# Seam between two attention stages: order of maxima, key loads and the last w2 products

## What is computed

```
h1 = tanh(einsum('bshd,do->bsho', t, w1) + b1)       # t: queries, keys; 16 heads of 16
prep = einsum('bsho,on->bshn', h1, w2) + b2          # the w2 products
...
s1 = einsum('bshe,bthe->bhst', q1, k1) / 4           # q1 = x wq1, k1 = ctx wk1, by head
s2 = einsum('bshe,bthe->bhst', q2, k2) / 4
attn = softmax(s1) - gain * softmax(s2)
o = einsum('bhst,bthe->bshe', attn, ctx wv)
```

## Time and profile before

| | us |
|---|---|
| median of 3 runs | 1492.02 |
| lowest, highest | 1490.94, 1496.18 |
| the profiled execution | 1488.99 |
| its span | 1487.2 |
| TensorE, VectorE, ScalarE, GpSimd busy | 1458.0, 1139.8, 823.4, 392.0 |

### The profile page before, as it was taken

How to read it: one execution, slowest core, us unless ns; L and a number is a source line. 1 busy time by engine, 2 the same in 40 slices (tenths; PEclk the granted TensorE clock), 3 DMA queues, 4 the chain that set the end, 5 groups by cost and what they waited for, 6 DMA issues and landing times.

```text
span 1487.2 us, 28701 instructions
## 1 busy us (share of the span) xinstructions
PE 1458.0 (98%) x11013; PEld 1042.6 (70%) x11013; DVE 1139.8 (77%) x2313; ACT 823.4 (55%) x1123; POOL 392.0 (26%) x426
## 2 busy tenths in 40 slices
PE   8999999999999999999999999999999999999998
PEld 5444444435666666666567888989989898888987
DVE  6445544378999999999967888788786878788686
ACT  5887888866888888888863431323232221222221
POOL 1000111224466677566364410000000000000001
PEclk9999999999999999999999999999999999999999
DMA  7766666557656656656642201010010101110001
GB/s 152 155 116 119 117 116 126 109 88 120 109 81 111 101 82 112 100 83 97 100 155 72 78 15 34 24 29 21 22 30 15 42 17 29 29 29 15 22 22 29
DMA packets 90092, 108.83 MB, mean 73 GB/s; under 512 B 18384, under 2 KB 58524, under 8 KB 89956
## 3 DMA queue, kind: packets, MB, share of 16 engines
q1 hardware_dynamic: 89624, 106.61, 38.0%
q10 hardware_dynamic: 332, 0.39, 0.1%
HBM read 26.00 MB, written 4.19 MB: 20 GB/s over the span
## 4 chain that ended last, share of the span: by engine, by line
PE 85%; DVE 6%; ACT 2%; SPq 2%; issue 2%; POOL 1%; DMA 1%; POOLq 0%; DVEq 0%; ACTq 0%
PE ps L109 82%; PE ps L1462 2%; SPq L119 2%; ACT PX L1634 1%; ACT H L708 1%; DVE NM L1692 1%; PE ps L1424 1%; PE ps L1470 1%; POOL X L1877 0%; PE ps L1395 0%; DVE GH L2585 0%; DVE GF L2579 0%; DVE GH L2583 0%; DMA ST<-QS 0%; DMA WS<-SM 0%
## 5 line engine op out<-in xcount | busy, mean ns | idle before, releaser
L1692 DVE TENSOR_REDUCE NM<-ps 128x4 f32<-128x1024 f32 x256 | 307.5, 1220 | 23.3 <-PE ps L109 22.4
L1634 ACT ACTIVATE PX<-ps 128x1024 f32<-128x1024 f32 x256 | 262.4, 1025 | 72.2 <-PE ps L109 70.4
L708 ACT ACTIVATE H<-ps 128x1024 f32<-128x1024 f32 x240 | 229.9, 1033 | 42.8 <-PE ps L109 40.7
L2354 ACT ACTIVATE GF<-ps,cols 128x512 f32<-128x512 f32 x128 | 87.3, 688 | 222.6 <-PE ps L109 209.1
L109 PE MATMUL ps<-XC,W_sw_w 128*128 128x512 f32 x768 | 187.1, 393 | 0.0
L109 PEld LDWEIGHTS ps<-XC,W_sw_w 128*128 128x128 f32 x768 | 140.0, 188 | 27.6
L2705 POOL TENSOR_SCALAR RSc<-AGc 128x4 f32<-128x4 f32 x23 | 6.0, 260 | 570.9 <-DVE AGc L2469 570.9
L2349 ACT ACTIVATE GF<-ps 128x512 f32<-128x512 f32 x64 | 38.2, 596 | 185.0 <-PE ps L109 185.0
L2585 DVE TENSOR_TENSOR GH<-GF,GH 128x512 fp32r<-128x512 f32 x192 | 133.9, 698 | 6.6
L109 PE MATMUL ps<-PX,VT 128*32 128x256 f32 x2048 | 137.0, 385 | 0.1
L109 PE MATMUL ps<-KT,QT 48*128 48x512 f32 x512 | 127.6, 495 | 1.7 <-DVE NM L1692 0.9
(11 more groups left out here) (261 smaller groups left out, 2521.2 us busy)
## 6 DMA issues: line engine op xcount, KB each, us to landing
KT<-KS SPq DMA_DIRECT2D x128, 192.0 KB, 4.7
ST<-QS SPq DMA_DIRECT2D x254, 96.0 KB, 2.8
QT<-XSb SPq DMA_DIRECT2D x128, 96.0 KB, 4.2
XR<-TT SPq DMA_DIRECT2D x352, 32.0 KB, 1.9
XT<-in_xT_dram SPq DMA_DIRECT2D x8, 512.0 KB, 4.4
raw_a<-in_x_dram SPq DMA_DIRECT2D x8, 512.0 KB, 4.3
CR<-in_ctxT_dram SPq DMA_DIRECT2D x8, 512.0 KB, 5.7
out_dram<-X SPq DMA_DIRECT2D x7, 512.0 KB, 2.9
```

The lines of the kernel that those rows point to most:

```text
L708: e.activation(H1[s % 8][:, :, :], PP[s % 3][:, :, :], ACT.Tanh, bias=0.0 if s > 15 else b1c[:, half:half + 1], scale=1.0).then_inc(act_th, 1)
L1634: e.activation(PX[s % 3][:, :, :, :], PP[2][:, :, :].rearrange("p g (c q) -> p g c q", c=2), ACT.Exp, bias=0.0, scale=0.25).then_inc(act_e ...
L1692: e.tensor_reduce(NM[u % 2][:, qc, :, :, i], PP[qc][:, :, :].rearrange("p g (m k) -> p g m k", m=2), AX.X, ALU.max, negate=True).then_inc( ...
L2354: e.activation(g[:, :], o, f, bias=cols[:, col:col + 1], scale=1.0).then_inc(act_g, 1)
```

## The change

- In the seam the maxima lead the scores by 12 steps up to step 0 (maxima(0) at -12), by 13 from step 1 to 4, by 14 from step 5. Steps 1 and 5 have two maxima each. The reductions follow the same order.
- LAST_W2 goes from -13 to -10: the last w2 products stand behind maxima(2). The three fillers of step -11 go. prep_v(0, 0) goes from -11 to -9, where prep_x(2) stands ahead of it. The second key product of block 1 goes from -13 to -11, behind maxima(1).
- Block 1 alone has its keys split by GpSimd: ScalarE copies the product to a new tile KR, GpSimd makes the high part, the rest and the copy; VectorE has no part in it. The waits of load, prep_k and ScalarE are counted accordingly.
- rows(0) goes from step -5 to -4. put_maxima(0) goes out at -3 with one DMA from SP; ScalarE issues the other, behind its own copy.
- The loads of block 1 go from steps -7, -4, -1, 2 to -3, -2, -1, 0, all behind put_maxima(0). ones_rows(1) goes from -6 to 5 and counts on another semaphore (d_w).

```diff
--- before.py
+++ after.py
@@ -171,7 +171,7 @@
 SOON_STEPS.update({J: 14 + 2 * (J - 74) for J in range(75, 87)})
 FIRST_STEP, LATER_STEP = -52, 39
-LAST_W2 = -13
+LAST_W2 = -10
 THREES_END = 56
@@ -1009,13 +1009,15 @@
 LEAD = 14
+SECOND_LOAD = -3
 SECOND_VALUES = (25, 29, 31, 33)
 NU = 4 * NP
 NB = 2 * NP
 NS = 8 * NU
 LAST_STEP = NS + 51
-
-BUSY = {-11: 3, -10: 1, -9: 1, -8: 1, -7: 1, -6: 1, -5: 1, -4: 2, -3: 1, -2: 1}
+OWN_KEYS = (0,) + tuple(range(2, 16))
+
+BUSY = {-10: 1, -9: 1, -8: 1, -7: 1, -6: 1, -5: 1, -4: 2, -3: 1, -2: 1}
 def phase_b(M, a_end):
@@ -1064,6 +1066,7 @@
     BN = [put(f"BNb{i}", [128, 4, 6]) for i in range(2)]
     AG = [put(f"AGb{i}", [128, 4, 2]) for i in range(2)]
     RS = [put(f"RSb{i}", [128, 4]) for i in range(2)]
+    KR = put("KR", [128, TOK])
     FB = Place(M, 0)("FB", [128, 9228])
     br = Place(M, 143360)("br", [128, 3, 256])
     cols, BC, Wce, Wme = M.cols, M.BC, M.Wce, M.Wme
@@ -1143,6 +1146,13 @@
     LATE = {NP - 2: 55, NP - 1: 87}
+    def maxima_due(s):
+
+        if s <= 0:
+            return (s + LEAD - 2,) if s >= 2 - LEAD else ()
+        first = s + LEAD - (2 if s < 2 else 1 if s < 6 else 0)
+        return range(first, min(NS, s + LEAD + 1 - (1 if s < 5 else 0)))
+
     def stats_due(s):
         for p, at in LATE.items():
@@ -1201,11 +1211,25 @@
         w.wait_ge(a_end["w1"], 16 * (n + 1))
+    def copied(B):
+
+        return B not in OWN_KEYS
+
+    def own(B):
+
+        return sum(2 for b in range(B) if not copied(b))
+
+    def parts(B):
+
+        return 2 * B + 4 * sum(1 for b in range(B) if copied(b))
+
     def k_due(s):
         for m in range(2):
             B = due(s, 8 * m - 37, 16, NB)
-            if B is not None and B != 2:
+            if B is not None and B != 2 and (B, m) != (1, 1):
                 return B, m
+            if s == -11:
+                return 1, 1
             if s == 3 + 4 * m:
                 return 2, m
         return None
@@ -1220,7 +1244,7 @@
                 return p, i
         if s in SECOND_VALUES:
             return 1, SECOND_VALUES.index(s)
-        return (0, 0) if s == -11 else None
+        return (0, 0) if s == -9 else None
     def out_due(s):
@@ -1244,7 +1268,7 @@
         return due(s, 2, 2, 4 * NU)
     def rows_due(s):
-        return due(s, -5, 8, NU)
+        return {-5: None, -4: 0}.get(s, due(s, -5, 8, NU))
     def turn_n_due(s):
         return NU - 1 if s == NS + 13 else due(s, 23, 8, NU - 1)
@@ -1278,7 +1302,7 @@
                 after_stack(w, 14)
             for g in range(2):
                 dma(e, f32(KT[i][64 * g + 48:64 * g + 52, :, :, :]).rearrange("r i m t -> r i (m t)"),
-                    f32(ones[:, :, :]).rearrange("r m t -> r (m t)").unsqueeze(1).to_broadcast([4, 4, 1024]), d_ones)
+                    f32(ones[:, :, :]).rearrange("r m t -> r (m t)").unsqueeze(1).to_broadcast([4, 4, 1024]), d_w if i else d_ones)
         def load(B, i):
             p, c = B // 2, B % 2
@@ -1288,8 +1312,8 @@
                 w.wait_ge(pe_g, 1)
             if B == 1:
                 after(w, "w2")
-            w.wait_ge(pool_ks, 2 * B + 2)
-            w.wait_ge(dve_ks, 2 * B + 2)
+            w.wait_ge(pool_ks, parts(B + 1))
+            w.wait_ge(dve_ks, own(B + 1))
             w.wait_ge(pe_st, 16 * (B - 2) + 8 + 2 * i + 2)
             k, q = KT[B % 2], QT[B % 2]
             for g in range(2):
@@ -1304,7 +1328,7 @@
             q, b = QT[u // 2 % 2], u % 2
             w.wait_ge(act_nr, u + 1)
             w.wait_ge(pe_st, 8 * (u - 4) + 8)
-            for g in range(2):
+            for g in range(2 if u else 1):
                 dma(e, f32(q[64 * g + 48:64 * g + 52, :, b, :]), f32(NR[u % 2][16 * g:16 * g + 16, :]), d_mr[u % 2])
         def load_fold():
@@ -1314,7 +1338,8 @@
             w.wait_ge(pe_v, 4 * NP)
             for name in T:
                 dma(e, T[name], a[name].rearrange("(c p) n -> p c n", c=2), d_T)
-            w.wait_ge(d_ones, 80)
+            w.wait_ge(d_ones, 48)
+            w.wait_ge(d_w, 64)
             for o, name in ((vb, "vb"), (vc, "vc"), (v2, "v2"), (br[:, :, :], "br"), (cols[:, :], "cols")):
                 dma(e, o, a[name], d_V)
             dma(e, BC[:, 0, :], a["BC"][:, 0, :], d_V)
@@ -1340,17 +1365,17 @@
         def step(s):
             if s == -33:
                 first_queries()
-            u = due(s, -4, 8, NU)
+            u = rows_due(s - 1)
             if u is not None:
                 put_maxima(u)
             p = ctx_due(s)
             if p is not None:
                 load_ctx(p)
             for i in range(4):
-                B = due(s, 3 * i - 23, 16, NB)
-                if B is not None:
+                B = 1 if s == i + SECOND_LOAD else due(s, 3 * i - 23, 16, NB)
+                if B is not None and (B != 1 or s == i + SECOND_LOAD):
                     load(B, i)
-            for i, at in enumerate((-16, -6)):
+            for i, at in enumerate((-16, 5)):
                 if s == at:
                     ones_rows(i)
             if s == NS - 28:
@@ -1381,7 +1406,7 @@
             w.wait_ge(pool_c, 4 * p + 2 * c + 2)
             w.wait_ge(*free[7])
             mm3(e, P[7], G[:, m, c, 0, :], G[:, m, c, 1, :], CH[p % 2][:, c, 0, :], CH[p % 2][:, c, 1, :], True, True).then_inc(pe_k, 1)
-            free[7] = (dve_ks, 2 * B + m + 1)
+            free[7] = (act_k, 2 * B + m + 1) if copied(B) else (dve_ks, own(B) + m + 1)
         def prep_x(B):
             p, c = B // 2, B % 2
@@ -1429,7 +1454,9 @@
             u, i, m = s // 8, s % 8 // 2, s % 2
             B, b = u // 2, u % 2
             k, q = KT[B % 2], QT[B % 2]
-            w.wait_ge(d_ones, 80)
+            w.wait_ge(d_ones, 48)
+            if B:
+                w.wait_ge(d_w, 64)
             w.wait_ge(d_mr[u % 2], 32 * (u // 2 + 1))
             w.wait_ge(act_ex, s)
             for kc in range(2):
@@ -1528,8 +1555,8 @@
         def step(s):
             busy(BUSY.get(s, 0))
-            if 0 <= s + LEAD < NS:
-                maxima(s + LEAD)
+            for t in maxima_due(s):
+                maxima(t)
             if s in (0, 1):
                 busy(2, 4 + 2 * s)
             if s == 2:
@@ -1596,6 +1623,9 @@
                 w.wait_ge(pe_rows, u + 1)
                 w.wait_ge(d_mr[u % 2], 32 * (u // 2))
                 e.activation(NR[u % 2][:, :], low[0:32, :], ACT.Copy).then_inc(act_nr, 1)
+                if u == 0:
+                    w.wait_ge(act_nr, 1)
+                    dma(e, f32(QT[0][112:116, :, 0, :]), f32(NR[0][16:32, :]), d_mr[0])
             B = x_due(s - 1)
             if B is not None:
                 w.wait_ge(pe_x, B + 1)
@@ -1619,9 +1649,13 @@
             if k is not None:
                 B, m = k
                 w.wait_ge(pe_k, 2 * B + m + 1)
-                for i in range(4):
-                    w.wait_ge(d_ld[B % 2][i], 64 * ((B - 2) // 2 + 1))
-                e.activation(KS[:, B % 2, 0, m, :], P[7], ACT.Copy).then_inc(act_k, 1)
+                if copied(B):
+                    w.wait_ge(pool_ks, parts(B) + 3 * m)
+                    e.activation(KR[:, :], P[7], ACT.Copy).then_inc(act_k, 1)
+                else:
+                    for i in range(4):
+                        w.wait_ge(d_ld[B % 2][i], 64 * ((B - 2) // 2 + 1))
+                    e.activation(KS[:, B % 2, 0, m, :], P[7], ACT.Copy).then_inc(act_k, 1)
             u = due(s, 14, 8, NU)
             if u is not None:
                 w.wait_ge(pool_oc, u + 1)
@@ -1685,8 +1719,7 @@
                 after(w, "combine")
                 e.tensor_tensor(PR[:, :, 8 * f:8 * f + 8, :], v7[:, :, :, 0:16],
                                 ZR[:, :, :, :].rearrange("p q h m -> p q (h m)").unsqueeze(3).to_broadcast([128, 2, 8, 16]), ALU.mult).then_inc(dve_pr, 1)
-            t = s + LEAD
-            if 0 <= t < NS:
+            for t in maxima_due(s):
                 u, i, qc = t // 8, t % 8 // 2, t % 2
                 w.wait_ge(pe_max, t + 1)
                 e.tensor_reduce(NM[u % 2][:, qc, :, :, i], PP[qc][:, :, :].rearrange("p g (m k) -> p g m k", m=2),
@@ -1704,7 +1737,7 @@
                 w.wait_ge(pool_on, u)
                 e.tensor_reduce(VR[:, :], OQ[:, :, :], AX.X, ALU.add).then_inc(dve_vr, 1)
             k = k_due(s - 1)
-            if k is not None:
+            if k is not None and not copied(k[0]):
                 B, m = k
                 w.wait_ge(act_k, 2 * B + m + 1)
                 e.tensor_tensor(KS[:, B % 2, 2, m, :], P[7], f32(KS[:, B % 2, 0, m, :]), ALU.subtract).then_inc(dve_ks, 1)
@@ -1830,8 +1863,16 @@
             if k is not None:
                 B, m = k
                 w.wait_ge(act_k, 2 * B + m + 1)
+                hi, again, lo = (KS[:, B % 2, l, m, :] for l in range(3))
                 one.wait()
-                one.done(e.tensor_copy(KS[:, B % 2, 1, m, :], f32(KS[:, B % 2, 0, m, :])), pool_ks)
+                if copied(B):
+                    for i in range(4):
```

(6 more changed lines are left out.)

## The result

| kernel | median us (lowest to highest) | ratio to before, 95% interval |
|---|---|---|
| before | 1492.8 (1489.66 to 1496.18) | |
| changed | 1496.22 (1493.62 to 1500.77) | 1.0022 [1.0015, 1.0029] |

The change costs 3.3 us by the ratio, 0.2%, with 20 runs on each side. The profiled execution of the changed kernel took 1496.26 with a span of 1494.3; the one of before took 1488.99 with 1487.2. These two differ by 7.3, which is more than the medians do, so the first question to the traces is which part of it belongs to the change.

The account below looks back on a forecast made before the run. TensorE was taken to carry most of the chain, with VectorE's reductions and SP's queue setting the seam up to step 8. A shift of +2.0 there on the median 1492.02 gave 1494.0, range 1489.2 to 1498.0.

Parts of the forecast that it names:

- The two idles: VectorE ahead of the first row of maxima, around 323.5 and 326: waits of 1.2 and 1.35 us.
- the signs against it: In the seam: first row issued before 331.5, a block 1 load under 0.85 us, or step 8's exponential before 353.8.
- Part 1: VectorE's reductions ahead of the first row of maxima: the row is asked for some 1.0 us later.
- Part 2: Lead of 12 at the first scores: step 0 at 338.1 instead of 338.66, nothing left by step 2.
- Part 3: SP's queue, first to second row: 16 loads at 1.0 us each, second row +2.4 us; +2.0 taken at step 8.
- the bound of +4.3: Upper bound for the second row's issue in SP's queue: 353.5, if 16 loads run at 1.12 us each.
- the upper price that I named: SP's issue time per load of block 1 at the pace of the slowest stretch: 1.12 us.
- Part 4: Covered work in the seam: GpSimd's keys cost nothing, ScalarE's issue (about 0.7 us) has room, ones have 10 us.
- What comes behind step 8 is TensorE's and isn't changed: TensorE behind step 8: the edit only shifts that step's start, and every microsecond there is one of the total.
- rival C: TensorE stands at steps 6 (1.5 us) and 8 (2 us), its clock falls: +7 beside the 2, 1501; chance 0.04.
- A: The lead pays in the seam: wait at step 8 gone, two reductions kept; -2.5 us, 1489.5; chance 0.30.
- B: No shift at step 8: SP's queue keeps its end, 349 to 350; 1492.0; chance 0.15.

Follow-up runs that it names:

- e4: Changed kernel with the first values product one step later (-8), apart from the transposes sharing its bank; ratio to before 1.0021.
- e3: Changed kernel with both DMAs of the second row of maxima issued by ScalarE behind its own copy; ratio to before 1.0024.
- e6: Changed kernel's order alone: keys, ones and first-row issues as in the kernel before, loads at -7, -3, -1, 2; ratio to before 1.0008.
- e2: Changed kernel with three fillers for TensorE ahead of the maxima and three ahead of the scores of step 8; ratio to before 1.0026.
- e8: e1 with the last ratio and exponential of the first stage one step later; ratio to before 1.0010.
- e9: Changed kernel with the step 8 fillers of e2 and the later ratio and exponential of e7; ratio to before 1.0024.
- e11: Kernel before with only half of the first row of maxima issued by ScalarE, the ones left at -6; ratio to before 0.9986.
- e1: Changed kernel with loads of block 1 at -7, -3, -1, 2, so four issues are ahead of the first row again; ratio to before 1.0008.
- e7: Changed kernel with the last ratio and exponential of the first stage one step later; ratio to before 1.0033.
- e5: Changed kernel with the whole order and load places of before; GpSimd's keys, ScalarE's half row and late ones kept; ratio to before 0.9987.
- e10: Kernel before with only the second buffer's rows of ones sent at step 5 instead of -6; ratio to before 0.9992.
- e12: e5 without the five fillers of steps 0, 1 and 2; ratio to before 0.9999.

## Why the prediction was right, and where its steps were not

The forecast was 1494.0 with 1489.2 to 1498.0; the median is 1496.22, inside the range, +3.3 by the ratio where +2.0 was forecast. Of the 2.2 between forecast and median, 0.8 are the kernel before itself (1492.8 with 20 runs, 1492.02 with three). There is luck in it: the range is 8.8 us wide and holds "no change" too, so that the median lies in it says little for the mechanism; the direction and the terms below say more. Of the signs named in advance, two failed: the scores of step 8 start at 356.26 and the second row is issued at 353.17, both less the 1.31 ahead of the seam, where 354.5 to 356 and 351.5 were named. The two idles and the waits for loads at steps 6 and 8 came as named, and none of the signs against it did.

**Part 1 held.** The first row was to be asked for 1.0 later; it is 1.07 later (13.83 against 12.76). Two idles of 1.2 and 1.35 were worked out; they are 1.04 and 1.58. e4 shows that the second is the shared bank's.

**Part 2 held.** Scores of step 0 were to start 0.56 earlier and do so by 0.66 (18.96 against 19.62); steps 1 and 2 start where they did, to 0.05. The lead of 12 gives nothing that lasts.

**Part 3 had the right mechanism and a term too small.** The sum gave +2.4 for the issue of the second row; it is +4.0, just inside the bound of +4.3. Of the missing 1.6, the 16 loads make 1.1 (17.1 instead of 16.0: the pace of the stretch, near the upper price that I named) and WS 0.3 (2.4 instead of 2.1). Against that the second row landed 3.09 after its issue instead of 4.15. The net at step 8 is +2.95 for my +2.0.

**Part 4 held** for GpSimd, which is done with the keys at 328.34 while the first load goes out at 334.98, and for the ones. ScalarE's issue of 0.75 lies where it has room; e3 shows what the same issue costs where it hasn't.

**The step that failed** is the sentence "What comes behind step 8 is TensorE's and isn't changed", with the sum's rule that every microsecond at step 8 is one of the total. The trace has +2.95 at step 8 and +4.50 at step 18. Two things were overlooked. First, WS stands in the same queue behind the same loads: I counted its 2.1 us of issue and not who waits for it. VectorE's reciprocal does, for 2.52 us, and its keys are late by that; the order of maxima alone also leaves VectorE late for them (1.23 in e6). In the changed kernel's own profile this cost nothing yet, as TensorE got there no sooner; it is what e2 ran into. Second, TensorE stands 1.39 and 1.21 us, with one pair of matmuls between, and its clock falls to 1.2 GHz for some 3 us. That is the mechanism of rival C. I had put its condition at a wait "well beyond 2 us", and its price at 7; none of the waits was that long, and the fall from step 8 to 9 cost 1.3 (2.99 - 1.67). The condition was the mistake: it was taken from the only fall that the trace of before has the earlier trace rows, and one long standstill says nothing about two short ones. These 1.3 are the larger part of the +1.55 that came between step 8 and step 18.

e2, e8 and e9 show that these two losses don't add up: whoever takes one away meets the other or a third. Taking both away in e9 left +2.88 at step 10, the shift of step 8 itself.

**Rivals.** A needed loads issued at under 0.85 each; they took 1.07, as the prose against it said. B needed SP's queue to keep its end; it moved by 4.0. The Trainium skill ("DMA: Bandwidth & Descriptors", Issuing engines are not separate DMA queues) was cited against more than one issue's worth from ScalarE's half. e11 agrees: one issue is spared, the backlog is not, and the second row gains 0.62.

**What stays open.** How the 3.3 us of time divide exactly. The profiles give 2.95 and 1.55 for one execution of each, which is more than the time shows. By the groups of ratios, the new order with early loads stands 1.2 to 1.5 us above the kernel before (0.0008 to 0.0010 of 1492), and the late loads add 1.6 to 3.7 (0.0011 to 0.0025); the intervals of e1, e6 and e8, some 0.15% to each side, are too wide for more. Why the clock stayed low for longer in e7 and e4 isn't explained either. Shown by time and trace together are two pairs: e7 and e8, apart only by the loads, and e5 and the changed kernel, with the same keys, ones and ScalarE half but the order and the place of the loads of before in e5, 0.9987 instead of 1.0022.

## What to carry to other kernels

When transfers are moved ahead of others in an in-order issue queue, multiply their number by the pace of the queue in that very stretch, and then look up who waits for each thing that now stands behind them; here the second row was priced and the wait for WS, directly ahead of it in the queue, was not. The long issue here (2.5 us instead of 0.6 to 0.8) was paying for what stood ahead of it: moving that (the ones, e10) brought the second row 1.9 us forward, moving the issue itself (e11) 0.6. Step 8 came 0.5 earlier in both, so the difference was not worth anything in this kernel. A shift on the critical path can cost more than its length, or a gain less, when the waits that it makes or takes away move the clock and the other engines' turns, so read the ten steps behind the point that moved as well.

## What was not expected of the hardware

TensorE's clock fell behind short waits: behind 1.39 and 1.21 us with one pair of matmuls between them in the changed kernel, during the second of 1.07 and 1.03 in e4, two us behind 0.69 and 1.51 in e7. A single one can go either way: after 1.24 in e1 it fell to 0.53, after 1.23 in e6 it stayed at 1.00 from 358 to 362. Ahead of the transposes of the first row the changed kernel, e1 and e6 all wait 1.03 to 1.06; in e6 alone the clock then falls, to 0.50 from 334 to 336. It fell in e12 also where only fillers had been taken out.

The spread of one kernel's runs goes with the clock. Of the 98 runs of the kernel before that stood beside e1 to e11, the 39 with a mean granted clock of 0.999 or more have a median of 1489.4 us and the 17 at 0.996 or less one of 1494.3; that is about 1.2 us for each 0.001. The changed kernel's runs have 0.9956 on the mean, those of before 0.9979, those of e5 0.9983 and of e11 0.9990. Runs at 0.993 or less, of 1497.2 to 1500.8 us, are 10 of the 114 of the nine kernels with the new order, and none of the 47 of e5, e10, e11 and e12 nor of the 115 of before whose clock is on record; why is not shown. Which of clock and time is the cause in such a pair is not shown by it, but a fall as at 20 to 25 us in one profile and not in the other is none of the change's (e5 has it, e1 hasn't), and has to be taken out before two profiles are compared.
